# Where the mixture's first weights are split: three attention runs of a four-layer stack

## The reference, cut to what matters

```
x = x + attention(xn) + mixture_of_experts(xn)     # layer 0: 16 heads with rotary, 32 experts, 4 chosen per row
x = x + selective_scan(xn) + spline_mlp(xn)        # layer 1
x = x + linear_recurrence(xn) + lookup_mlp(xn)     # layer 2
x = x + attention(xn) + mixture_of_experts(xn)     # layer 3: 16 heads with biases, 8 experts, 2 chosen per row
```

```
q, k, v = xn @ Wq[h], xn @ Wk[h], xn @ Wv[h]       # (+ biases in layer 3, rotary on q and k in layer 0)
p   = softmax(mask(q @ k.T / sqrt(128)))
out = out + (p @ v) @ Wo[h]

w, idx = top_k(softmax(router(xn)));  w = w / sum(w)
y = sum over the chosen experts e of w[e] * ((act(xn @ gate[e]) * (xn @ up[e])) @ down[e])
```

## Time and profile before

| what | value |
|---|---|
| time, median of 3 runs (lowest to highest) | 1683.09 us (1680.79 to 1683.25) |
| profiled execution: its time, its span | 1679.66 us, 1676.8 us |
| granted TensorE clock, mean over the span | 0.971 |
| busy: PE, PE weight loads, DVE, ACT, POOL | 92%, 72%, 70%, 57%, 42% |
| page: median us from issue to landing, a head's load (384 KB) | 3.1 |
| the same, a group of experts (1152 KB in layer 0, 768 KB in layer 3) | 5.3, 4.3 |
| the mixture's first two loads of the second rotary run are issued at | 523.68 us, 0.5 us behind head 15's load |

### The profile page before, as it was taken

The page is one execution under the profiler, slowest core; times in us unless marked ns, Lnnn a source line. Parts: engine busy times, 40 slices in busy tenths (PEclk is TensorE's granted clock), DMA queues, the critical chain, the costliest instruction groups (busy, mean ns, idle before and its releaser), DMA issues. The chain is left out here.

```text
span 1676.8 us, 26441 instructions
## 1 busy us (share of the span) xinstructions
PE 1534.9 (92%) x8400; PEld 1213.5 (72%) x8400; DVE 1165.6 (70%) x2620; ACT 952.9 (57%) x2076; POOL 704.0 (42%) x686
## 2 busy tenths in 40 slices
PE   6999989979999798999989988979998997999898
PEld 4777779957877798555535546668887885888787
DVE  5888866658888667899889964446667344666733
ACT  6667656846665466676476532246655444666543
POOL 5999943333221234099639760122122222222222
PEclk9999999999999899999999989899999998999999
DMA  3212122111112121150050000011112112111121
GB/s 123 88 61 80 66 95 94 36 55 35 50 50 83 60 95 61 41 189 1 1 204 27 0 7 5 3 58 42 50 34 76 57 38 71 51 41 44 66 66 42
DMA packets 34333, 98.36 MB, mean 59 GB/s; under 512 B 6388, under 2 KB 11256, under 8 KB 32072
## 3 DMA queue, kind: packets, MB, share of 16 engines
q1 hardware_dynamic: 33064, 90.95, 16.2%
q0 software_dynamic: 1184, 6.37, 1.1%
HBM read 96.12 MB, written 1.18 MB: 58 GB/s over the span
## 5 line engine op out<-in xcount | busy, mean ns | idle before, releaser
L921 POOL TENSOR_TENSOR head_low<-head,head_high 128x512 fp32r<-128x512 f32 x64 | 81.8, 1277 | 451.6 <-ACT head_high L911 450.8
L1928 POOL TENSOR_TENSOR experts_low<-experts,experts_high 128x1536 fp32r<-128x1536 f32 (+3 forms) x56 | 126.5, 2260 | 251.9 <-ACT experts_high L1878 95.8
L1305 ACT ACTIVATE probs<-banks,neg_max 128x512 f32<-128x512 f32 (+3 forms) x256 | 133.6, 525 | 59.0 <-DVE neg_max L1188 53.4
L2473 POOL TENSOR_TENSOR rings<-du,bc_rows 128x512 f32<-128x512 f32 x124 | 155.7, 1279 | 20.9 <-DMA bc_rows<-bc_rows 14.4
L2399 DVE TENSOR_TENSOR_SCAN banks<-banks,rings 128x512 f32<-128x512 f32 x128 | 155.9, 1220 | 3.0 <-POOL rings L2473 2.0
L1570 DVE SCALAR_TENSOR_TENSOR hidden<-banks,weight,act_out 128x96 f32<-128x96 f32 (+1 forms) x192 | 62.7, 367 | 127.2 <-ACT act_out L1538 127.1
L1538 ACT ACTIVATE act_out<-banks 128x256 f32<-128x256 f32 (+2 forms) x112 | 47.4, 423 | 174.4 <-PE banks L225 174.2
L2191 PE MATMUL banks<-rings,ident 128*128 128x512 f32 x256 | 126.2, 607 | 16.5 <-DVE rings L2422 16.2
L225 PE MATMUL banks<-experts_high,xnT_high 128*128 128x384 f32 (+1 forms) x384 | 139.8, 364 | 1.0 <-PEq L187 1.0
L225 PE MATMUL banks<-experts_low,xnT_high 128*128 128x384 f32 (+1 forms) x384 | 138.1, 360 | 0.0
L225 PE MATMUL banks<-experts_high,xnT_low 128*128 128x384 f32 (+1 forms) x384 | 138.1, 360 | 0.0
(11 more groups left out here) (305 smaller groups left out, 4739.6 us busy)
## 6 DMA issues: line engine op xcount, KB each, us to landing
head<-in_heads SPq DMA_DIRECT2D x64, 384.0 KB, 3.1
experts<-in_experts SPq DMA_DIRECT2D x16, 1152.0 KB, 5.3
bc_rows<-bc_rows SPq DMA_DIRECT2D x30, 512.0 KB, 6.1
experts<-in_experts SPq DMA_DIRECT2D x16, 768.0 KB, 4.3
values<-in_values SPq DMA_DIRECT2D x32, 256.0 KB, 3.2
coef<-in_spline_coef POOLq DMA_DIRECT2D x8, 768.0 KB, 4.7
idx<-in_lut_idx SPq DMA_DIRECT2D x16, 134.0 KB, 2.1
x<-in_x SPq DMA_DIRECT2D x2, 512.0 KB, 4.5
```

What stands on the lines that cost most here:

```text
L1305: last = nc.scalar.activation(prob_tile(i), score_tile(i), ACT.Exp, bias=neg_max[:, i:i + 1], scale=QK_SCALE, accum_out=row_sum[:, i:i + 1])
L1928: nc.gpsimd.tensor_tensor(parts[gpar][1][:, columns], raw[gpar][:, columns], parts[gpar][0][:, columns].bitcast(FP32), ALU.subtract)\
L2473: nc.gpsimd.tensor_tensor(inflow[:, step % INFLOWS], du[:, c], B_of(n), ALU.mult)\
```

## The change

In the three merged runs (a rotary one, two biased ones):

- SyncE issues the loads of groups 0 and 1 ahead of the reloads for heads 14 and 15 instead of behind them (`load_pair`).
- ScalarE splits group 0 behind head 12 and the gate/up part of group 1 behind head 13 (`first_high` and `second_high` at `h == HEADS - 4` and `HEADS - 3`), instead of behind head 14 and inside head 15.
- GpSimd makes group 0's gate/up low part once head 13's tiles are scaled (`probs_ready` 14), behind `low_qk(15)` and ahead of `low_wo(14)`; group 0's down part and group 1's gate/up part once head 14's tiles are scaled (`probs_ready` 15), ahead of `low_wo(15)`. Two waits are added on GpSimd.

The same instructions run before and after; none is added or removed beside the two waits. TensorE's and VectorE's streams are unchanged.

```diff
@@ attention, sync
         with sp.Fori(0, HEADS // LOOP - 1) as i:
             for c in range(LOOP):
                 reload(LOOP * i + c, c, 2 * i + c // 2)
+        if ahead and ahead.load_pair:
+            ahead.load_pair(sp)
         for h in range(HEADS - LOOP, HEADS - 2):
             reload(h, h % LOOP, h // 2)
@@ attention, scalar
         for h in range(HEADS - LOOP, HEADS - 1):
             head(h, h % LOOP, h // LOOP)
-        if ahead:
+            if ahead and ahead.low_pair and h == HEADS - 4:
+                ahead.first_high(act)
+            if ahead and ahead.low_pair and h == HEADS - 3:
+                ahead.second_high(act)
+        if ahead and not ahead.low_pair:
             ahead.first_high(act)
         exponentials(HEADS - 1)
         if spline:
             scale_wide(HEADS - 1)
-        if ahead and ahead.second_high:
+        if ahead and ahead.second_high and not ahead.low_pair:
             ahead.second_high(act)
         store_turned(HEADS - 1)
@@ attention, gpsimd
         def lows(h, c, pair):
             low_qk(pool, h + 2, c % 2)
+            if ahead and ahead.low_pair and isinstance(h, int) and h == HEADS - 3:
+                pool.wait_ge(probs_ready.sem, probs_ready.at(HEADS - 2))
+                ahead.low_pair[0](pool)
             if c % 2 == 0 and not (isinstance(pair, int) and pair + 2 >= PAIRS):
                 low_values(pool, pair + 2, c // 2 % 2)
             low_wo(pool, h + 1, 1 - c % 2)
...
+        if ahead and ahead.low_pair:
+            pool.wait_ge(probs_ready.sem, probs_ready.at(HEADS - 1))
+            ahead.low_pair[1](pool)
         low_wo(pool, HEADS - 1, 1)
@@ mixture
+    def load_pair(sp):
+        for g in range(2):
+            load(sp, g, g)
...
         for g in range(2):
-            if started and g == 0:
+            if merged or started and g == 0:
                 continue
-            load(g, g)
+            load(sp, g, g)
...
+    def low_behind(pool):
+        low_down(pool, 0, 0)
+        low_gu(pool, 1, 1)
+
     def gpsimd(pool):
...
-        if not started:
+        if not started and not merged:
             start.low_first(pool)
-        low_gu(1, 1)
+        if not merged:
+            low_gu(pool, 1, 1)
...
-    ahead = Ahead(start.load_router, start.route, start.begin_vector, start.choose, start.first_high, second_high)
+    ahead = Ahead(start.load_router, start.route, start.begin_vector, start.choose, start.first_high, second_high,
+                  load_pair=load_pair, low_pair=(lambda pool: low_gu(pool, 0, 0), low_behind))
```

More of the change, by code:

```diff
@@ L1587, in __init__ @@
     def __init__(self, load, route, begin_vector, choose, first_high, second_high=None, load_first=None,
-                 low_first=None, exponent=None, weigh=None):
+                 low_first=None, exponent=None, weigh=None, load_pair=None, low_pair=None):
         self.load, self.route, self.begin_vector, self.choose = load, route, begin_vector, choose
@@ L1591, in __init__ @@
         self.load_first, self.low_first, self.exponent, self.weigh = load_first, low_first, exponent, weigh
+        self.load_pair, self.low_pair = load_pair, low_pair
 class MixtureStart:
@@ L1761, in mixture, with load @@
     norm_phase = lambda n: n - (ITEMS - norm.phases + 1) if isinstance(n, int) else -1
+    def load(sp, g, gpar):
+        sp.dma_start(raw[gpar][:], head_rows(experts_dram, g)).then_inc(experts_loaded[gpar].sem, 16)
+    def load_pair(sp):
+        for g in range(2):
+            load(sp, g, g)
     def sync(sp):
-        def load(g, gpar):
-            sp.dma_start(raw[gpar][:], head_rows(experts_dram, g)).then_inc(experts_loaded[gpar].sem, 16)
         if not merged and not started:
@@ L1787, in sync @@
                 sp.wait_ge(down_split.sem, down_split.at(g + 1))
-                load(g + 2, gpar)
+                load(sp, g + 2, gpar)
                 if table:
@@ L1922, in scalar, with low, low_gu, low_down @@
             norm.scalar(act, norm.phases - 1)
-    def gpsimd(pool):
-        def low(columns, high, split, g, gpar):
-            pool.wait_ge(high.sem, high.at(g + 1))
-            nc.gpsimd.tensor_tensor(parts[gpar][1][:, columns], raw[gpar][:, columns],
-                                    parts[gpar][0][:, columns].bitcast(FP32), ALU.subtract)\
-              .then_inc(split.sem, 1)
-        def low_gu(g, gpar):
-            if table and not (isinstance(g, int) and g < 2):
-                pool.wait_ge(table.chain.sem, table.chain.at(table.LINKS * (g - 1) + 4))
-            low(slice(0, GU), gu_high, gu_split, g, gpar)
-        low_down = lambda g, gpar: low(slice(GU, GU + R * D), down_high, down_split, g, gpar)
-        if not started:
+    def low(pool, columns, high, split, g, gpar):
+        pool.wait_ge(high.sem, high.at(g + 1))
+        nc.gpsimd.tensor_tensor(parts[gpar][1][:, columns], raw[gpar][:, columns],
+                                parts[gpar][0][:, columns].bitcast(FP32), ALU.subtract)\
+          .then_inc(split.sem, 1)
+    def low_gu(pool, g, gpar):
+        if table and not (isinstance(g, int) and g < 2):
+            pool.wait_ge(table.chain.sem, table.chain.at(table.LINKS * (g - 1) + 4))
+        low(pool, slice(0, GU), gu_high, gu_split, g, gpar)
+    def low_down(pool, g, gpar):
+        low(pool, slice(GU, GU + R * D), down_high, down_split, g, gpar)
+    def low_behind(pool):
+        low_down(pool, 0, 0)
+        low_gu(pool, 1, 1)
+    def gpsimd(pool):
+        if not started and not merged:
             start.low_first(pool)
-        low_gu(1, 1)
+        if not merged:
+            low_gu(pool, 1, 1)
         with pool.Fori(0, GROUPS // 2 - 1) as i:
-            low_down(2 * i + 1, 1)
-            low_gu(2 * i + 2, 0)
-            low_down(2 * i + 2, 0)
-            low_gu(2 * i + 3, 1)
-        low_down(GROUPS - 1, 1)
+            low_down(pool, 2 * i + 1, 1)
+            low_gu(pool, 2 * i + 2, 0)
+            low_down(pool, 2 * i + 2, 0)
+            low_gu(pool, 2 * i + 3, 1)
+        low_down(pool, GROUPS - 1, 1)
         if norm and norm.with_xm:
```

## The result

The changed kernel took 1656.3 us (median of 4 runs, 1653.54 to 1661.41) against 1681.94 us before (1675.81 to 1683.25): ratio 0.9877, interval 0.9854 to 0.99. So the change makes the kernel about 1% faster; 0.9906 of the 1683.09 us at the start is 1667.3, and the three ratios together say 15 to 21 us.

What follows compares the result with a forecast made beforehand. GpSimd's batch beside head 15's softmax was taken to bound head 15, holding VectorE's two-column negation and scalings. Savings of 9.0 + 4.3 + 4.15 = 17.45 us from 1683.1 gave 1665.6 us, range 1661 to 1674.

Steps and rivals of the forecast that it cites:

- The slower rival: GpSimd's long parts also hold VectorE instructions with one PSUM operand: 20 us lost against 17.45 saved, 1687 us; chance 0.03.
- Rotary end, 9.0 us: Head 15 of the second rotary run: 6.1 us from an earlier turn plus 2.9 us from the clock staying up.
- head 13 late: Rotary run: ScalarE's split of group 0 starts head 13's exponentials late; 0.3 us taken, bounds 0 and 0.78.
- head 14: Rotary run: VectorE's two-column negation meets `low_wo(14)` and loses about 0.4 us; bounds 0 and 3.45.
- the wait: Rotary head 15: TensorE's turn starts at 549.4 instead of 555.53, saving 6.1 us.
- the clock: Rotary head 15, turn to `yT`: 4.22 us at full clock instead of 7.11, saving 2.9 us.
- Biased ends, 4.3 and 4.15 us: Head 15 of the two biased runs: `yT` comes 4.3 us earlier in the first, 4.15 in the second.
- the product with v: Biased head 15: starts at 1297.15 behind `choose` and a low part, then runs 2.56 us until `yT`.
- Loads: Loads issued three reloads, about 23 us, earlier cost 0; the other bound was 0 to 2.2 us in a run.
- The clock did not stay low: Rival for head 15: the clock stays low in the shorter gaps, so only 13.1 us are saved, 1670; chance 0.12.
- The collision: Rival: GpSimd's first part holds head 14's negation and scaling, some 8 us lost again, 1673.5; chance 0.09.
- Nothing was given back: Rival: the mixture's start is bound by something that doesn't move, so the saving is given back, 1683; chance 0.03.

Runs made afterwards that it cites:

- highs_early: The changed kernel with loads and ScalarE's parts early but GpSimd's low parts in one batch as in the kernel before; ratio to the kernel before 0.9998.
- lows_late: The kernel before with one more wait, so GpSimd's whole batch starts only once head 15's tiles are scaled; ratio 0.9943.
- no_second_wait: The changed kernel without GpSimd's wait for head 14's scaled tiles; ratio to the kernel before 0.9954.
- filler: The kernel before with unread matmuls (27 rotary, 15 biased) put into TensorE's wait of head 15; 1667.93 us in a single run.
- biased_only: The new order in the two biased runs only, the rotary run as in the kernel before; ratio to the kernel before 0.9949.
- thirds_choose: The changed kernel with `choose` behind the turned tiles' low parts, and ScalarE's and GpSimd's early work in thirds; ratio to the kernel before 0.9876, 1658.69 us.
- after_third: The changed kernel unaltered, timed a third time; ratio to the kernel before 0.9908.

## Why the prediction was right

- *The cause.* That GpSimd's batch holds VectorE's negation and scalings in head 15, and that this bounds the head, held. highs_early keeps everything but the batch's place and saves nothing; lows_late moves the batch alone and frees the softmax; no_second_wait takes the stall to head 14.
- *Which instructions are held.* One-column negations, reductions and instructions with one PSUM operand were not held, as read from one row each. The slower rival, worked out from the opposite, has no support: 1.23 and 1.21 us under a running part.
- *Rotary end, 9.0 us.* The two profiled executions give 19.15 + 10.99 + 11.46 - 9.50 - 11.23 - 11.74 = 9.13. Its terms came out singly too: head 13 late by 0.28 (0.3 taken), head 14 by 0.24 through `low_wo(14)` (0.4 taken), the wait 6.8 less these two, 6.2 (6.1 taken), the clock 2.8 by filler (2.9 taken). That the clock's term came out so closely is partly luck: both figures are from the same profiled execution before, and against the 18.30 of biased_only the term is 1.95 and the end 8.3.
- *Biased ends, 4.3 and 4.15 us.* 4.8 and 4.7. The step that was mis-sized is the product with v: 2.56 us were taken from head 14, a stretch that holds a wait of its own for a low part (0.19 us by its row); in head 15, with all low parts of the tiles one behind the other, it is 1282.67 - 1280.54 = 2.13. That `choose` would be late next was right (0.51 us of waiting, and 0.36 won by moving it).
- *Loads.* They went out at 497.58 us instead of 523.68, two reloads earlier and not three, as the prediction has it; the 23 us are right. The term of 0 held: in thirds_choose, with the loads as early, head 13 is back at 11.46.
- *The other rivals.* The clock did not stay low in the changed kernel (1.00), though it was 0.83 and 0.84 in the second biased end of biased_only and thirds_choose. The collision did move to head 14, but only for `low_wo(14)`'s rest. Nothing was given back behind `yT` (5.15 us before and after: 1309.12 - 1303.97 before).
- *The sum.* 18.6 us in the traces where 17.45 were forecast; 15 to 21 in the times. What was missed is the spread of the median: the range took 2.3 us for it, and executions of one program differ by 8 to 11 us (1653.54 to 1661.41, in after_third 1658.08 to 1669.08), in the two traces compared above through the clock in stages far from the change.

## What to carry to other kernels

When a VectorE instruction that is usually 0.2 or 0.8 us long shows 2 or 3, look at what GpSimd has running and whether the two end together; then move the GpSimd work to where VectorE's instructions have a PSUM operand, and guard it with a wait on VectorE's last scaling, because without that wait it slides onto the next softmax. A wait alone, in the right place, gave about half of the gain here. Count also what the stand-still does to the matmul clock behind it: in the rotary end that was 2 to 2.8 us of 8.3 to 9.1, and it varied from one execution to the next where the wait did not.

## What the runs showed of the hardware that was not expected

- Two GpSimd parts in direct succession hold a pair of VectorE scalings for almost both their lengths: 5.45 us for 0.82 us of work (no_second_wait), 5.41 in highs_early. In narrower windows of the no_second_wait timeline the pair is 1.96 us from 536.29, its end 0.29 behind that of the 768-column part (537.96), and 3.57 us from 538.17, its end 0.22 behind that of the 1536-column part (541.52): VectorE did not get both scalings in between the two.
- A 32-column subtraction with two SBUF inputs is held as a scaling is (1.93 against 0.19 us; in the rotary run of lows_late, with 128 columns, 2.94 against 0.29), while MAX8 and memset beside the same GpSimd part are not.
- The same program's granted clock in an untouched stage was 0.92 in one execution and 0.84 in another, and the span differed by 10.6 us, nearly all of it around that stage.
- The granted clock was also low without a long stand-still: 0.84 over 11 us in which TensorE was busy for 10.45 (thirds_choose), 0.69 behind a wait of 0.56 us (no_second_wait). That the waits of 4 to 7 us bring the low stretch of the old order is shown by filler; what brings these is open.
